# Normalising with the mean itself in place of its negative, in a fused attention and expert layer

## The chip, the cores and the metric

The kernel runs on one core of one Trainium2 chip. The time is the device time of one execution in microseconds (us), and smaller is better. The core has five engines with instruction queues of their own: PE (TensorE, matrix products), DVE (VectorE), ACT (ScalarE), POOL (GpSimd) and SP (SyncE, here a DMA queue only). They meet in semaphores: an instruction can wait until a semaphore has reached a value, and add to one when it ends.

## The reference

One layer for 8 sequences of 512 tokens with 256 features, float32. The attention is unusual: the softmax weights of a token are multiplied by its own value row, so their sum, computed as a ratio that is close to 1, scales the value rows. The feed-forward part picks one of 8 low-rank adapters per token. There are four normalisations without weights.

```python
def _layernorm(x, axis=-1, eps=1e-05):
    m = jnp.mean(x, axis=axis, keepdims=True)
    v = jnp.var(x, axis=axis, keepdims=True)
    return (x - m) / jnp.sqrt(v + eps)

# attention (16 heads)
att = jax.nn.softmax(jnp.einsum('blhd,bmhd->blmh', q, k) * scale, axis=2)
opt = jnp.einsum('blmh,blhd->blhd', att, v).reshape(b, l, d)
return opt @ w_out.T + b_out

# feed-forward: for each expert i of 8, masked to the tokens whose gate picks it
lora = jnp.einsum('bsr,fr->bsf', jnp.einsum('bsd,rd->bsr', x, lora_A[i]), lora_B[i])
inter = jax.nn.relu(base + lora)
expert_out = jnp.einsum('bsf,df->bsd', inter, wo_W) + wo_b

# the layer
x = x + _layernorm(attn(_layernorm(x)))
x = x + _layernorm(ffn(_layernorm(x)))
```

## The kernel before

A batch is one sequence: 4 tiles (t) of 128 tokens by 256 features. The program is a pipeline over 8 batches, written out by hand for each engine. In batch b every engine goes through 32 slots. A slot is one pair of score tiles: PE multiplies (L222) two 128x512 tiles into two of five PSUM banks (`ps`), DVE takes the negative row maximum (L722), ACT does the exponential and its sum (L511). Between the slots stand pieces of the other stages, for batches b+1 (projections), b-1 and b-2 (what follows the attention). Large products are made of three float32 rounded ones, from a high and a low part of each operand (`three`, L189). PE works strictly in the order of its program, with three further banks (`pu`).

The normalisations are shared out. DVE computes mean and variance per token: `bn_stats` by tile (L758) and `bn_aggr` (L763), into `mv[n][:, t, 0]` (mean) and `mv[n][:, t, 1]` (variance). POOL then runs `spread` (L996): it writes the negative mean into `nmr[n][:, 0]` (L1001), the variance plus epsilon into `nmr[n][:, 1]` (L1002), and that to the power -0.5 into `nmr[n][:, 2]` (L1004). After it `norm` (L1007) works tile by tile: (src + negative mean) * power, with both as per-partition scalars (L1010). One spread serves two or four tiles.

Norm 0 is that of x (`x_norm`, giving `xn`), 1 that of the attention's output (`y_norm`, added to `xb` by L1016), 2 that of the sum (`sum_norm`, giving `y`), 3 that of the feed-forward output (`y2_norm`). In each batch POOL's order (L1138) is: scale the value rows `vo` of batch b-1 by the ratio that DVE made from the finished exponentials (L1047), two low parts of `inter` (L1079, L1081), `x_norm(b+1)`, `y_norm(b-1)` for tiles 0, 1 and then 2, 3, `sum_norm(b-1)` in the same halves, bias additions, the mask of the gate, `y2_norm(b-2)`, two more low parts.

Who waits for these norms: PE transposes the result of norm 2 in `y_t` (L276) at slot 14, by the helper at L227, ahead of all later work in its queue, and ACT and DVE make high and low parts from it (L544, L726). DVE's statistics of the sum wait for POOL's additions (L797). In the last batch `y_half` (L343) does the transposes by half batches (L336), the norms of its second half and of the end are done by DVE itself (L880, L883), and only their spreads stay on POOL (L1148 to L1150); DVE waits for them. In the first batch DVE and POOL share the spread of norm 0 (L896, L1117), and DVE subtracts the mean (L899).

Of the kernel before, what the change touches and what calls it, by code (L numbers as in the profile page):

```python
# [8 lines left out]
ALU = mybir.AluOpType  # L9
# [4 lines left out]
NT = L // 128  # L14
EPS = 1e-5
# [17 lines left out]
def sandwich(nc, x, wqk, wv, bqk, wout, wgate, wi, lora, wib, wo, bfree, bg, ident, out):  # L33
    with ExitStack() as ctx:
        def sb(name, shape, dt=F32):
            return ctx.enter_context(nc.sbuf_tensor(name, shape, dt))

        def sem(name):
            return ctx.enter_context(nc.semaphore(name))
# [4 lines left out]
        xb = sb("xb", [128, XB, NT, D])  # L44
        xn = sb("xn", [128, NT, D])
# [24 lines left out]
        halves = sb("halves", [128, NT])  # L70
# [4 lines left out]
        sone = sb("sone", [128, NT, H])  # L75
        st6 = [sb(f"st6_{i}", [128, NT, 6]) for i in range(3)]
        mv = [sb(f"mv_{i}", [128, NT, 2]) for i in range(3)]
        nmr = [sb(f"nmr_{i}", [128, 3, NT]) for i in range(3)]
        gs = sb("gs", [128, NT, 40])
        g8 = sb("g8", [128, 6, NT, E])  # L80
        g1 = sb("g1", [128, 5, NT])
# [45 lines left out]
        rstd = [sem(f"rstd{i}") for i in range(4)]  # L127
# [589 lines left out]
        def vector(e):  # L717
# [160 lines left out]
                whole_stats(3, 2, B - 1, (t,))  # L878

            def norm(i, n, dst, src, b, ts):  # L880
                e.wait_ge(rstd[i], (6 if i in (1, 2) else 3) * b + 3 + 3 * (ts[0] // len(ts)))
                for t in ts:
                    e.tensor_scalar(dst[:, t, :], src[:, t, :], nmr[n][:, 0, t:t + 1], nmr[n][:, 2, t:t + 1], ALU.add,  # L883
                                    ALU.mult).then_inc(normed[i], 1)

            def add(i, src, b, ts):
# [6 lines left out]
                tile_stats(0, 0, xb[:, 0], t)  # L893
            whole_stats(0, 0, 0, ALL)
            e.wait_ge(stats[0], 8)
            e.tensor_scalar(nmr[0][:, 1, :], mv[0][:, :, 1], EPS, None, ALU.add).then_inc(rstd[0], 2)  # L896
            e.wait_ge(rstd[0], 3)
            for t in ALL:
                e.tensor_scalar(xn[:, t, :], xb[:, 0, t, :], mv[0][:, t, 0:1], nmr[0][:, 2, t:t + 1], ALU.subtract,  # L899
                                ALU.mult).then_inc(normed[0], 1)  # L900
            e.wait_ge(bqk_loaded, 16)
            e.tensor_scalar(bqk_s[:, 0:2], bqk_s[:, 0:2], 0.25, None, ALU.mult).then_inc(qk_split, 1)
# [44 lines left out]
            b = B - 1  # L947
# [34 lines left out]
            slot(29)  # L982
            slot(30), ratio_half(1), gate_half(1, 0), gate_half(2, 0)
            slot(31), project(b, 1), gate_half(3, 0), y_stats(b, HALVES[1]), norm(1, 1, y, y, b, HALVES[1])
            add(1, y, b, HALVES[1]), sum_stats(b, HALVES[1]), norm(2, 1, y, xb[:, b % XB], b, HALVES[1])
            y_half(1), gate_half(1, 1), gate_half(2, 1), gate_half(3, 1), f1_half(0, 0), f1_half(0, 1)
            y2_stats(b - 1, HALVES[0]), f1_half(0, 2), f1_half(0, 3), f1_half(1, 0), y2_stats(b - 1, HALVES[1])
            f1_half(1, 1), f1_half(1, 2), f1_half(1, 3), last_stats(0), last_stats(1), last_stats(2)
            norm(3, 2, y2, y2, b, (0,)), add(3, y2, b, (0,)), norm(3, 2, y2, y2, b, (1,)), add(3, y2, b, (1,))
            last_stats(3), norm(3, 2, y2, y2, b, (2,)), add(3, y2, b, (2,)), norm(3, 2, y2, y2, b, (3,))  # L990
            add(3, y2, b, (3,))
# [3 lines left out]
        def pool(e):  # L995
            def spread(i, n, b, ts=ALL):  # L996

                s = slice(ts[0], ts[-1] + 1)
                k = (6 if i in (1, 2) else 3) * b + 3 * (ts[0] // len(ts))
                e.wait_ge(stats[i], 8 * b + 2 * ts[-1] + 2)  # L1000
                e.tensor_scalar(nmr[n][:, 0, s], mv[n][:, s, 0], -1.0, None, ALU.mult).then_inc(rstd[i], 1)  # L1001
                e.tensor_scalar(nmr[n][:, 1, s], mv[n][:, s, 1], EPS, None, ALU.add).then_inc(rstd[i], 1)  # L1002
                e.wait_ge(rstd[i], k + 2)
                e.tensor_tensor(nmr[n][:, 2, s], nmr[n][:, 1, s], halves[:, s], ALU.pow).then_inc(rstd[i], 1)  # L1004
                return k + 3

            def norm(i, n, dst, src, b, ts=ALL):  # L1007
                e.wait_ge(rstd[i], spread(i, n, b, ts))
                for t in ts:
                    e.tensor_scalar(dst[:, t, :], src[:, t, :], nmr[n][:, 0, t:t + 1], nmr[n][:, 2, t:t + 1], ALU.add,  # L1010
                                    ALU.mult).then_inc(normed[i], 1)

            def add(i, src, b, ts=ALL):
# [24 lines left out]
            def x_norm(b):  # L1038
                if here(b):
                    if b:  # L1040
                        e.wait_ge(xnT_ps, 2 * b)
                    norm(0, 0, xn, xb[:, b % XB], b)
# [41 lines left out]
            def y_norm(b, ts):  # L1084
                if here(b):
                    norm(1, 1, y, y, b, ts), add(1, y, b, ts)

            def sum_norm(b, ts):
                if here(b):
                    norm(2, 1, y, xb[:, b % XB], b, ts)  # L1090
# [22 lines left out]
            for i in range(PIECES):  # L1113
                e.memset(stack[:, i, 0:2].rearrange("p q c l -> p (q c l)").bitcast(F32), 0.0).then_inc(zeroed, 1)
            e.wait_ge(const_set, CONSTS)
            e.wait_ge(rstd[0], 2)
            e.tensor_tensor(nmr[0][:, 2, :], nmr[0][:, 1, :], halves[:], ALU.pow).then_inc(rstd[0], 1)  # L1117
            e.wait_ge(normed[0], 4)
            first_piece(e, 0, 1)
            first_piece(e, 1, 1)  # L1120
# [21 lines left out]
            b = B - 1  # L1142
# [3 lines left out]
            v_bias(b), scale_half(0), y2_bias(b - 2, 1), mask(b - 1), y2_norm(b - 2), y_norm(b, HALVES[0])  # L1146
            f1_lows(b - 1, 0, 0), sum_norm(b, HALVES[0]), f1_lows(b - 1, 0, 1), f1_lows(b - 1, 1, 0)
            scale_half(1), f1_lows(b - 1, 1, 1), mask_half(0), spread(1, 1, b, HALVES[1])  # L1148
            spread(2, 1, b, HALVES[1]), y2_bias(b - 1, 0), mask_half(1), y2_bias(b - 1, 1), y2_norm(b - 1)
            spread(3, 2, b, (0,)), spread(3, 2, b, (1,)), spread(3, 2, b, (2,)), spread(3, 2, b, (3,))  # L1150

# [84 lines left out]
        @block.vector  # L1236
        def _(e):
            vector(e)

        @block.gpsimd  # L1240
        def _(e):
            pool(e)
# [50 lines left out]
```

## Time and profile before

| | us |
|---|---|
| median of 3 runs | 541.47 |
| lowest and highest | 539.78, 541.62 |
| the profiled execution | 541.58 |
| its span, first to last instruction | 539.8 |

| engine | busy us | share | instructions |
|---|---|---|---|
| PE | 508.2 | 94% | 2721 |
| DVE | 463.9 | 86% | 991 |
| ACT | 453.5 | 84% | 1238 |
| POOL | 368.7 | 68% | 557 |

All rows come from the one profiled execution. A row "A <- B" says that A stood idle until B ended. "issue" in a chain is time in which an engine waited for nothing that the profile shows, such as the gap between two instructions that follow each other. "xN" behind an operation merges N instructions in sequence, and the time is that of them all. The mean granted TensorE clock is 0.991 of full speed. Consecutive matmuls overlap, and their ends are modelled.

### The profile page before, as it was taken

The numbers are of one execution on the slowest core, as the hardware profiler recorded it, in microseconds if no ns is written. First come the engines' busy times: TensorE is split into PE (matmuls) and PEld (weight loads), VectorE is DVE, ScalarE is ACT, GpSimd is POOL, SyncE is SP. The second block draws the span as 40 slices with busy tenths as digits, with TensorE's granted clock in tenths as the row PEclk, the third lists the DMA queues.
The fourth block names the chain that finished last, engine by engine and source line by source line (L and its number), as shares of the span: only waits on it lengthen the run. The fifth ranks groups of instructions, "written<-read, shape, count | busy, mean of one in ns | idle before, by whom it ended". The sixth has DMA issues, their size and how long they took to land.

```text
span 539.8 us, 8865 instructions
## 1 busy us (share of the span) xinstructions
PE 508.2 (94%) x2721; PEld 403.4 (75%) x2721; DVE 463.9 (86%) x991; ACT 453.5 (84%) x1238; POOL 368.7 (68%) x557
## 2 busy tenths in 40 slices
PE   8999988999999999999999999999999998798995
PEld 6765544588887789677877788778878787577995
DVE  4598999988999899998999899998999789975455
ACT  2499988999889998999889998999889988893220
POOL 5696046417992898559991998379873987797263
PEclk9989999999999999999999999999999999998998
DMA  7693453035310625045411633053403640310002
GB/s 240 187 251 92 110 125 79 1 88 147 76 42 2 166 74 153 1 109 126 118 40 34 172 76 111 0 148 88 118 1 80 156 117 1 78 40 1 1 2 79
DMA packets 22645, 47.63 MB, mean 88 GB/s; under 512 B 5220, under 2 KB 13540, under 8 KB 21958
## 3 DMA queue, kind: packets, MB, share of 16 engines
q1 hardware_dynamic: 21910, 45.95, 32.0%
q0 software_dynamic: 256, 0.52, 0.4%
q10 hardware_dynamic: 432, 0.59, 0.3%
q8 instruction: 22, 0.36, 0.3%
q14 instruction: 25, 0.20, 0.1%
HBM read 8.24 MB, written 4.19 MB: 23 GB/s over the span
## 4 chain that ended last, share of the span: by engine, by line
POOL 32%; PE 29%; ACT 24%; DVE 7%; issue 5%; POOLq 0%; ACTq 0%
ACT ps L511 17%; PE pu L193 15%; POOL y L1010 7%; PE ps L222 6%; POOL nmr L1004 5%; POOL inter L1081 5%; POOL xb L1016 4%; PE ps L193 3%; POOL vo L1047 3%; DVE nmax L722 3%; ACT qk L525 3%; POOL xn L1010 2%; POOL inter L1079 2%; POOL nmr L1002 2%; POOL nmr L1001 2%
## 5 line engine op out<-in xcount | busy, mean ns | idle before, releaser
L511 ACT ACTIVATE ps<-ps,nmax 128x512 f32<-128x512 f32 x512 | 344.7, 699 | 20.2 <-DVE nmax L722 19.8
L722 DVE TENSOR_REDUCE nmax<-ps 128x1 f32<-128x512 f32 x512 | 320.0, 679 | 25.9 <-PE ps L222 24.6
L222 PE MATMUL ps<-stack 128*128 128x512 f32 x512 | 176.8, 420 | 3.6 <-ACT ps L511 2.6
L511 ACT ACTIVATION_READ_ACCUMULATOR ps<-ps,nmax 128x1 f32 x512 | 125.9, 246 | 0.0
L222 PEld LDWEIGHTS ps<-stack 128*128 128x128 f32 x512 | 94.2, 190 | 36.1 <-ACT ps L511 23.1
L193 PE MATMUL pu<-yT,wi_r 128*128 128x512 f32 x336 | 87.9, 397 | 0.0
L193 PE MATMUL pu<-wo_r,inter 128*128 128x256 f32 x624 | 80.9, 282 | 0.0
L193 PEld LDWEIGHTS pu<-wo_r,inter 128*128 128x128 f32 x624 | 78.9, 188 | 2.6
L193 PEld LDWEIGHTS pu<-yT,wi_r 128*128 128x128 f32 x336 | 62.8, 188 | 13.5
L1081 POOL TENSOR_TENSOR inter<-y,inter 128x1024 fp32r<-128x1024 f32 x26 | 62.1, 2387 | 2.1
L200 PE MATMUL ps<-ones_r 128*128 128x512 f32 x115 | 48.6, 470 | 6.8 <-ACT ps L511 5.6
L193 PE MATMUL pu<-xnT,wqk_r 128*128 128x512 f32 x192 | 49.5, 395 | 0.7 <-DVE xnT L726 0.7
L200 PEld LDWEIGHTS ps<-ones_r 128*128 128x128 f32 x115 | 23.0, 202 | 31.2 <-ACT ps L511 25.2
L1024 POOL TENSOR_TENSOR ml<-gs,g 128x128 f32<-128x128 f32 (+1 forms) x9 | 3.5, 389 | 62.2 <-DVE g L865 62.2
L1004 POOL TENSOR_TENSOR nmr<-nmr,halves 128x2 f32<-128x2 f32 (+2 forms) x50 | 39.8, 796 | 4.2
L1016 POOL TENSOR_TENSOR xb<-xb,y 128x256 f32<-128x256 f32 x58 | 41.1, 735 | 1.8
L193 PEld LDWEIGHTS pu<-xnT,wqk_r 128*128 128x128 f32 x192 | 35.5, 188 | 8.2 <-issue 1.1
L1047 POOL TENSOR_TENSOR vo<-vo,sone 128x256 f32<-128x256 f32 x32 | 18.9, 623 | 29.0 <-DVE sone L816 24.7
L271 PE MATMUL pu<-wout_s,oT 128*128 128x256 f32 x128 | 34.5, 395 | 2.3 <-ACT oT L581 1.6
L1001 POOL TENSOR_SCALAR nmr<-mv 128x2 f32<-128x2 f32 (+2 forms) x50 | 12.0, 240 | 33.0 <-DVE mv L763 29.9
L1079 POOL CAST inter<-y 128x1024 fp32r<-128x1024 f32 x26 | 27.0, 1039 | 10.6 <-ACT y L576 10.6
L576 ACT ACTIVATE y<-pu 128x512 f32<-128x512 f32 x52 | 33.8, 677 | 0.1
(130 smaller groups left out, 685.2 us busy)
## 6 DMA issues: line engine op xcount, KB each, us to landing
stack<-qk SPq DMA_DIRECT2D x256, 128.0 KB, 2.5
xb<-in_x SPq DMA_DIRECT2D x7, 512.0 KB, 4.9
out_y<-xb SPq DMA_DIRECT2D x7, 512.0 KB, 3.6
xb<-in_wo SPq DMA_DIRECT2D x1, 1024.0 KB, 7.6
vo<-in_wi SPq DMA_DIRECT2D x2, 512.0 KB, 6.8
oT<-in_wqk ACTq DMA_DIRECT2D x1, 512.0 KB, 4.1
xb<-in_x SPq DMA_DIRECT2D x4, 128.0 KB, 4.1
stack<-qk SPq DMA_DIRECT2D x8, 64.0 KB, 2.4
```

What stands on the lines that cost most here:

```text
L193: p = e.matmul(out_, lT(a, c), r(b_, c), start=first and n == 0 and j == 0, stop=last and n == len(chunks) - 1 and j == 2)
L200: e.matmul(bank[:].rearrange("p (k m) -> p k m", k=4), ones_r[:], ones_r[:].unsqueeze(1).to_broadcast([128, 4, 128]), start=True, stop=True)
L222: e.matmul(ps[i % NS][:], st[:, 1 - p, c, t * 128:(t + 1) * 128], st[:, 2, c, :], start=True, stop=True).then_inc(scored, 1)
L271: p = e.matmul(o, oT[:, c, t * 128:(t + 1) * 128], wout_s[:, c, :], start=c == 0, stop=c == 1)
L511: e.activation(ps[i % NS][:], ps[i % NS][:], ACT.Exp, bias=nmax[:, i % 8:i % 8 + 1], accum_out=ssum[:, b % 2, t, h:h + 1]).then_inc(exped, 1)
L722: e.tensor_reduce(nmax[:, i % 8:i % 8 + 1], ps[i % NS][:], AX_X, ALU.max, negate=True).then_inc(maxed, 1)
L1004: e.tensor_tensor(nmr[n][:, 2, s], nmr[n][:, 1, s], halves[:, s], ALU.pow).then_inc(rstd[i], 1)
L1010: e.tensor_scalar(dst[:, t, :], src[:, t, :], nmr[n][:, 0, t:t + 1], nmr[n][:, 2, t:t + 1], ALU.add, ALU.mult).then_inc(normed[i], 1)
L1016: e.tensor_tensor(xb[:, b % XB, t, :], xb[:, b % XB, t, :], src[:, t, :], ALU.add).then_inc(added[i], 1)
L1047: e.tensor_tensor(vt, vt, sone[:, t, :].unsqueeze(2).to_broadcast([128, H, 16]), ALU.mult).then_inc(scaled, 1)
L1079: e.tensor_copy(high, whole).then_inc(f1_pool_high, 1)
L1081: e.tensor_tensor(inter[:, 1, f:f + 2, :], whole, high.bitcast(F32), ALU.subtract).then_inc(f1_pool_low, 1)
```

## The change

POOL no longer writes the negative mean. `nmr` has two rows in place of three (variance plus epsilon, power), each spread has two operations in place of three, and the norms on POOL and on DVE's tail take `mv[n][:, t, 0:1]` as their first scalar and subtract. The semaphore values of `rstd` follow: two steps per spread in place of three.

```diff
-        nmr = [sb(f"nmr_{i}", [128, 3, NT]) for i in range(3)]
+        nmr = [sb(f"nmr_{i}", [128, 2, NT]) for i in range(3)]
...
             def norm(i, n, dst, src, b, ts):
-                e.wait_ge(rstd[i], (6 if i in (1, 2) else 3) * b + 3 + 3 * (ts[0] // len(ts)))
+                e.wait_ge(rstd[i], (4 if i in (1, 2) else 2) * b + 2 + 2 * (ts[0] // len(ts)))
                 for t in ts:
-                    e.tensor_scalar(dst[:, t, :], src[:, t, :], nmr[n][:, 0, t:t + 1], nmr[n][:, 2, t:t + 1], ALU.add,
+                    e.tensor_scalar(dst[:, t, :], src[:, t, :], mv[n][:, t, 0:1], nmr[n][:, 1, t:t + 1], ALU.subtract,
                                     ALU.mult).then_inc(normed[i], 1)
...
-            e.tensor_scalar(nmr[0][:, 1, :], mv[0][:, :, 1], EPS, None, ALU.add).then_inc(rstd[0], 2)
-            e.wait_ge(rstd[0], 3)
+            e.tensor_scalar(nmr[0][:, 0, :], mv[0][:, :, 1], EPS, None, ALU.add).then_inc(rstd[0], 1)
+            e.wait_ge(rstd[0], 2)
...
             def spread(i, n, b, ts=ALL):
 
                 s = slice(ts[0], ts[-1] + 1)
-                k = (6 if i in (1, 2) else 3) * b + 3 * (ts[0] // len(ts))
+                k = (4 if i in (1, 2) else 2) * b + 2 * (ts[0] // len(ts))
                 e.wait_ge(stats[i], 8 * b + 2 * ts[-1] + 2)
-                e.tensor_scalar(nmr[n][:, 0, s], mv[n][:, s, 0], -1.0, None, ALU.mult).then_inc(rstd[i], 1)
-                e.tensor_scalar(nmr[n][:, 1, s], mv[n][:, s, 1], EPS, None, ALU.add).then_inc(rstd[i], 1)
-                e.wait_ge(rstd[i], k + 2)
-                e.tensor_tensor(nmr[n][:, 2, s], nmr[n][:, 1, s], halves[:, s], ALU.pow).then_inc(rstd[i], 1)
-                return k + 3
+                e.tensor_scalar(nmr[n][:, 0, s], mv[n][:, s, 1], EPS, None, ALU.add).then_inc(rstd[i], 1)
+                e.wait_ge(rstd[i], k + 1)
+                e.tensor_tensor(nmr[n][:, 1, s], nmr[n][:, 0, s], halves[:, s], ALU.pow).then_inc(rstd[i], 1)
+                return k + 2
 
             def norm(i, n, dst, src, b, ts=ALL):
                 e.wait_ge(rstd[i], spread(i, n, b, ts))
                 for t in ts:
-                    e.tensor_scalar(dst[:, t, :], src[:, t, :], nmr[n][:, 0, t:t + 1], nmr[n][:, 2, t:t + 1], ALU.add,
+                    e.tensor_scalar(dst[:, t, :], src[:, t, :], mv[n][:, t, 0:1], nmr[n][:, 1, t:t + 1], ALU.subtract,
                                     ALU.mult).then_inc(normed[i], 1)
```

POOL's program around `x_norm` and the first half of `y_norm`, before; the shapes are partitions x elements of what is written:

```order
L1001 TENSOR_SCALAR nmr<-mv 128x4 [waits stats0,xnT_ps]
L1002 TENSOR_SCALAR nmr<-mv 128x4
L1004 TENSOR_TENSOR nmr<-nmr,halves 128x4 [waits rstd0]
L1010 TENSOR_SCALAR xn<-xb,nmr 128x256 [waits rstd0]
L1010 TENSOR_SCALAR xn<-xb,nmr 128x256 x3
L1001 TENSOR_SCALAR nmr<-mv 128x2 [waits stats1]
L1002 TENSOR_SCALAR nmr<-mv 128x2
L1004 TENSOR_TENSOR nmr<-nmr,halves 128x2 [waits rstd1]
L1010 TENSOR_SCALAR y<-y,nmr 128x256 [waits rstd1]
L1010 TENSOR_SCALAR y<-y,nmr 128x256
```

The same place now (all lines from here on are one lower):

```order
L1001 TENSOR_SCALAR nmr<-mv 128x4 [waits stats0,xnT_ps]
L1003 TENSOR_TENSOR nmr<-nmr,halves 128x4 [waits rstd0]
L1009 TENSOR_SCALAR xn<-xb,mv,nmr 128x256 [waits rstd0]
L1009 TENSOR_SCALAR xn<-xb,mv,nmr 128x256 x3
L1001 TENSOR_SCALAR nmr<-mv 128x2 [waits stats1]
L1003 TENSOR_TENSOR nmr<-nmr,halves 128x2 [waits rstd1]
L1009 TENSOR_SCALAR y<-y,mv,nmr 128x256 [waits rstd1]
L1009 TENSOR_SCALAR y<-y,mv,nmr 128x256
```

L1001 is now the addition of epsilon, which was L1002, and takes over the wait for DVE's statistics. The norm reads `mv` beside `nmr`. POOL's program has 50 instructions fewer; no other order changes. At its end, where DVE waits for the spread of each of the last four tiles, it was

```order
L1001 TENSOR_SCALAR nmr<-mv 128x1 [waits stats3]
L1002 TENSOR_SCALAR nmr<-mv 128x1
L1004 TENSOR_TENSOR nmr<-nmr,halves 128x1 [waits rstd3]
L1001 TENSOR_SCALAR nmr<-mv 128x1 [waits stats3]
L1002 TENSOR_SCALAR nmr<-mv 128x1
L1004 TENSOR_TENSOR nmr<-nmr,halves 128x1 [waits rstd3]
```

and is now

```order
L1001 TENSOR_SCALAR nmr<-mv 128x1 [waits stats3]
L1003 TENSOR_TENSOR nmr<-nmr,halves 128x1 [waits rstd3]
L1001 TENSOR_SCALAR nmr<-mv 128x1 [waits stats3]
L1003 TENSOR_TENSOR nmr<-nmr,halves 128x1 [waits rstd3]
```

so that the power is the second instruction after the wait instead of the third.

## Rows read from the trace of the kernel before

**Rows 1.** The profile's page, parts 1 and 4: busy time by engine; shares of the chain.
```profile
PE 508.2 (94%) x2721; PEld 403.4 (75%) x2721; DVE 463.9 (86%) x991; ACT 453.5 (84%) x1238; POOL 368.7 (68%) x557
...
POOL 32%; PE 29%; ACT 24%; DVE 7%; issue 5%; POOLq 0%; ACTq 0%
```

**Rows 2.** The chain that ended last, 190 to 250 us: start, length (us), what.
```profile
191.18 2.36 POOL vo L1047 x4
...
200.51 0.24 POOL nmr L1001
200.76 0.09 issue
200.84 0.25 POOL nmr L1002
...
215.52 0.23 POOL nmr L1001
...
216.97 1.11 POOL y L1010 x2
218.08 0.14 issue
```

**Rows 3.** PE in order of time, three stretches: start, length (us), line, operation.
```profile
216.27 1.10 PE L222 MATMUL ps<-stack 128*128 128x512 f32 x4
218.21 1.06 PE L227 MATMUL pu<-id_s,y 128*128 128x128 f32 x8 [0.85 <-POOL y L1010]
...
483.02 0.63 PE L336 MATMUL pu<-id_s,y 128*128 128x128 f32 x4 [0.20 <-POOL y L1010]
...
505.20 0.63 PE L336 MATMUL ps<-id_s,y 128*128 128x128 f32 x4 [0.35 <-DVE y L883]
```

**Rows 4.** Who waited for whom: total us, times, longest.
```profile
PE pu L227 <- POOL y L1010: 5.0, 7, 0.9
```

**Rows 5.** One line's instructions: the POOL operation that negates the mean, ns min/median/max.
```profile
L1001 POOL TENSOR_SCALAR nmr<-mv x50: 221/239/297, 33.0 to 535.0; 128x2 f32<-128x2 f32 x32, 128x4 f32<-128x4 f32 x14, 128x1 f32<-128x1 f32 x4
```

**Rows 6.** DVE in order of time, two stretches of the same batch.
```profile
206.95 0.25 DVE L763 BATCH_NORM_AGGREGATE mv<-st 128x2 f32<-128x6 f32 x2
...
212.15 0.43 DVE L758 BATCH_NORM_STATS2 st<-xb 128x6 f32<-128x256 f32 x1 [0.40 <-POOL xb L1016]
212.83 0.43 DVE L758 BATCH_NORM_STATS2 st<-xb 128x6 f32<-128x256 f32 x1 [0.26 <-POOL xb L1016]
213.29 0.25 DVE L763 BATCH_NORM_AGGREGATE mv<-st 128x2 f32<-128x6 f32 x2
```

**Rows 7.** Busy us (x count) of PE, PEld, DVE, ACT, POOL, one batch's period; then clock.
```profile
190.24:249.53 59.29, 58.06 (x319) 47.20 (x318) 55.16 (x119) 55.93 (x155) 45.15 (x67) 1.00 0.34 90
```

**Rows 8.** The end of the chain, from 535 us: start, length (us), what.
```profile
535.00 0.28 POOL nmr L1001
...
535.36 0.38 POOL nmr L1002
...
535.78 0.61 POOLq L34
...
536.41 0.42 DVE y L883
```

**Rows 9.** DVE in order of time, near the end.
```profile
535.24 0.42 DVE L889 TENSOR_TENSOR xb<-xb,y 128x256 f32<-128x256 f32 x1
```

**Rows 10.** POOL's groups by shape: busy us, mean ns, idle before.
```profile
L1081 POOL TENSOR_TENSOR inter<-y,inter 128x1024 fp32r<-128x1024 f32 x26 | 62.1, 2387 | 2.1
L1016 POOL TENSOR_TENSOR xb<-xb,y 128x256 f32<-128x256 f32 x58 | 41.1, 735 | 1.8
L1010 POOL TENSOR_SCALAR y<-y,nmr 128x256 f32<-128x256 f32 x58 | 31.7, 559 | 2.4
...
L1106 POOL TENSOR_TENSOR wi_r<-vo,wi_r 128x512 fp32r<-128x512 f32 x4 | 5.0, 1282 | 0.0
```

**Rows 11.** ACT in order of time, at the eviction of yT.
```profile
218.88 1.09 ACT L544 ACTIVATE yT<-pu 128x512 fp32r<-128x512 f32 x2 [0.97 <-PE pu L227]
```

More of the change, by code:

```diff
@@ L895, in vector @@
             e.wait_ge(stats[0], 8)
-            e.tensor_scalar(nmr[0][:, 1, :], mv[0][:, :, 1], EPS, None, ALU.add).then_inc(rstd[0], 2)
-            e.wait_ge(rstd[0], 3)
+            e.tensor_scalar(nmr[0][:, 0, :], mv[0][:, :, 1], EPS, None, ALU.add).then_inc(rstd[0], 1)
+            e.wait_ge(rstd[0], 2)
             for t in ALL:
-                e.tensor_scalar(xn[:, t, :], xb[:, 0, t, :], mv[0][:, t, 0:1], nmr[0][:, 2, t:t + 1], ALU.subtract,
+                e.tensor_scalar(xn[:, t, :], xb[:, 0, t, :], mv[0][:, t, 0:1], nmr[0][:, 1, t:t + 1], ALU.subtract,
                                 ALU.mult).then_inc(normed[0], 1)
@@ L1115, in pool @@
             e.wait_ge(const_set, CONSTS)
-            e.wait_ge(rstd[0], 2)
-            e.tensor_tensor(nmr[0][:, 2, :], nmr[0][:, 1, :], halves[:], ALU.pow).then_inc(rstd[0], 1)
+            e.wait_ge(rstd[0], 1)
+            e.tensor_tensor(nmr[0][:, 1, :], nmr[0][:, 0, :], halves[:], ALU.pow).then_inc(rstd[0], 1)
             e.wait_ge(normed[0], 4)
```

## The prediction

> **What bounds the kernel now.** I read the page's shares first. PE is busy for 94% of the span, and yet the chain that ended last lies on POOL for 32% of it, more than on any other engine [rows 1]. So PE is nearly full, but something on POOL is waited for. The next view is therefore the chain in order of time, over one batch in the middle of the run (190 to 250 us). It lies on POOL without a break from the scaling of vo at 191.18 to the last normalised y tile: 216.97 + 1.11 = 218.08 us, and then 0.14 us to PE [rows 2]. After that it goes through ACT and PE to the next scaling of vo at 250.48, so one period is about 59.3 us. The third view is PE in order of time around the hand-over: PE's score matmuls end at 217.37 (216.27 + 1.10), and its transposes of y start at 218.21, after 0.85 us of idle time that POOL's norm ended [rows 3]. The list of waits has the same stall for the whole run: 7 times, 5.0 us, 0.9 at most [rows 4]. Two more such stalls stand in the last batch, where the program uses the half transposes: 0.20 us at 483.02 and 0.35 us at 505.20, the last one behind a norm on DVE that itself waits for POOL's statistics [rows 3].
>
> So two loops of nearly equal length run side by side. The one through POOL is now the longer by 0.85 us per batch. The other is PE's own work.
>
> **What the change removes.** It takes out the operation that negates the mean, 50 times [rows 5]. One costs 0.24 us of busy time, but what the chain loses is the distance from its start to the start of the next operation: 200.84 - 200.51 = 0.33 us with the 0.09 us of issue behind it [rows 2]; over the spreads of one batch it is 0.32 on average. The 50 of them are 16 us of POOL's time. Most of this is worth nothing by itself, since only five of the six per batch lie between the scaling of vo and the transposes of y: one of x_norm, two of y_norm, two of sum_norm. They make 5 x 0.325 = 1.62 us, and the norm that PE waits for ends at 218.08 - 1.62 = 216.46 us in place of 218.08, or 216.60 at PE.
>
> Does each of the five count in full? The first operation of a spread waits for DVE's statistics, so POOL could arrive too early. The last spread is the tightest. POOL comes to it at 215.52 now and would come at 215.52 - 4 x 0.325 = 214.22. The aggregates it reads are done at 213.29 + 0.25 = 213.54 [rows 2, 6], which leaves 0.68 us, and they come earlier too, as DVE's statistics there waited 0.40 and 0.26 us for POOL's additions [rows 6]. For the second half of y they are done at 206.95 + 0.25 = 207.20 [rows 6], and POOL comes to that spread at about 208.1. So no new wait for DVE appears, and all 1.62 us arrive.
>
> **What is late next.** PE gets to the transposes at 217.37 and POOL's tile would be there at 216.60. The stall of 0.85 us goes wholly, and 0.77 us of POOL's saving is over. From here PE decides. Its busy time in this period of 59.29 us is 58.06 [rows 7], so 1.23 us is all the idle time it has, 0.85 of them this stall. The gain of a batch is therefore at least 0.85 us, if PE's own loop is untouched, and at most 1.23 us. For the part above 0.85 speaks that DVE no longer stands 0.66 us at its statistics [rows 6], so that ACT gets its maxima sooner and PE its free banks; against it that PE runs nearly back to back before 217.37. I take it close to the lower end, 0.07 us in each of five steady batches, 0.35 us in all; the ends are 0 and 5 x 0.38 = 1.9 us.
>
> **The last batch.** The two stalls of the half transposes are 0.20 and 0.35 us [rows 3]. POOL saves three spreads ahead of the first and DVE's norms get theirs two spreads sooner (0.65 us) ahead of the second, so both go, and no more than the stall does, 0.55 us together. At the very end nothing runs beside the chain: POOL negates the mean at 535.00, starts the epsilon operation at 535.36, then the power, and DVE's norm starts at 536.41 [rows 8]. The removed step is worth 535.36 - 535.00 = 0.36 us if the rest keeps its length. The epsilon operation took 0.38 us there, against 0.25 in the middle of the run [rows 2, 8], while DVE's addition with two operands in SBUF ran at 535.24 to 535.66 [rows 9]. With the step gone, it is the power that starts beside that addition and may be stretched in the same way. I take 0.30, with ends at 0.1 and 0.4.
>
> The Trainium skill has a rule for this (SBUF — State Buffer, Who interferes with whom): a DVE instruction with two SBUF inputs contends with a GpSimd instruction that reads SBUF. By that rule the power would be held until 535.66, and the final step would bring about 0.1 us less than 0.36; without it all 0.36. Either leaves the forecast where it is.
>
> **Other edits, at nothing.** The norms read the mean where DVE wrote it, still a per-partition scalar, and subtract in place of adding: same count, same shapes. The buffer of statistics gets smaller. On DVE the first batch's semaphore steps change by number only. No DMA and no instruction of PE, ACT, DVE or SP moves.
>
> **The sum.** 5.0 (seven stalls) + 0.35 (relief) + 0.55 (half transposes) + 0.30 (end) = 6.2 us. The profiled execution took 541.58 us, 0.1 us above the median of 541.47, so 541.58 - 6.2 = 535.4 us. By the bounds alone it runs from 5.0 + 0 + 0.55 + 0.1 = 5.65 to 5.0 + 1.9 + 0.55 + 0.4 = 7.85 us of gain: 535.9 to 533.7. Three runs of the same kernel here lie 1.8 us apart, which I add on either side.
>
> **Rivals.**
> (a) The subtraction costs more on POOL than the addition. No row shows POOL's two-step operation with a subtraction. For equal cost speaks that its two-operand subtraction goes by 2387 - 1282 = 1105 ns for 512 more elements, 2.16 ns each; from 1282 ns at 512 that line gives 730 ns at 256, and the addition of 256 took 735 [rows 10]. Twelve normalised tiles lie in the POOL stretch, so the change would lose from 1.62 / 12 = 0.135 us more per tile, 24% over the 559 ns of now [rows 10]. If the tile cost what the two-operand form costs, 735 in place of 559 ns, 12 x 0.176 = 2.11 us would come against 1.62 saved: 0.49 us longer in each of the six to seven periods, some 3 us in all, 544.5 us. Slower than before. The lower bound is no difference.
> (b) Another engine takes most of the stall. ACT stands 0.97 us before the eviction of y [rows 11] and then runs without idle time, and the chain goes over ACT's exponentials until about 228 us. If these hold PE back as soon as it comes earlier, half of the 5.0 us comes: 2.5 + 0.55 + 0.3 = 3.3 us, 538.3 us. Against it: ACT's queue starts at that eviction, and moves with it.
> (c) All of POOL's saving arrives: five batches at 1.62, 0.4 and 0.3 for the first and the last stall, 0.85 for the end: 9.7 us, 531.9 us. This needs PE to arrive 0.77 us sooner as well, and PE has 0.38 us of other idle time per batch [rows 7], so its busy time would have to hide waits.
>
> **Chances.** The forecast (533.7 to 537.5) 0.70; (b) 0.14; (c) 0.07; (a) 0.06; 0.03 for what I do not see. The measurement tells 0.5%, 2.7 us, from no change: faster is below 538.8 us. The forecast, (c) and nearly half to two thirds of (b) lie there: 0.86. Within 0.5%: the rest of (b) and the cheap end of (a), 0.09. Slower: 0.05. For 8 in 10 I go from 533.0 to 538.9 us, which takes in the forecast and most of (b) and leaves out (a) and (c).
>
> **What would show it.** The wait of PE's transposes for POOL's norm falls from 5.0 us to under 0.5. The distance between two scalings of vo falls from 59.3 to 58.3 or 58.4 us. POOL's busy time falls by 12 us and its normalised tiles stay at 0.56 us; at over 0.69 us I would be wrong by (a). DVE's waits for POOL's additions (0.40, 0.26) vanish. If PE's wait for POOL goes and the period stays above 58.9, it is (b), and a new wait of PE for ACT must show. If POOL waits for DVE's aggregates inside the stretch, my margins of 0.7 us were wrong.

## The result

The changed kernel takes 602.66 us (median of 4 runs, 600.23 to 604.06) against 541.37 us for the kernel before (539.78 to 541.62). The ratio is 1.113, with a 95% interval of 1.110 to 1.115. My forecast was 535.4 us, in a range of 533.0 to 538.9 us, with 0.05 for any slowdown. It missed by 67 us, on the wrong side. The medians below leave out two executions that lie far from the others of their kernels, 700.27 us (mean granted clock 0.65) where DVE negates and 2828.37 us where PE is kept busy.

From the page of the changed kernel: busy time by engine, and the chain's shares, which answer to [rows 1].

```profile
PE 530.2 (88%) x2721; PEld 413.9 (69%) x2721; DVE 469.2 (78%) x991; ACT 456.9 (76%) x1238; POOL 433.4 (72%) x507
...
POOL 47%; PE 20%; DVE 17%; ACT 10%; issue 5%; POOLq 0%; ACTq 0%
```

POOL has 50 instructions fewer and 64.7 us more busy time (433.4 against 368.7). The groups by shape say where it went (busy us, mean ns; idle before); they answer to [rows 10].

```profile
L1009 POOL TENSOR_SCALAR y<-y,mv,nmr 128x256 f32<-128x256 f32 x58 | 70.5, 1227 | 2.3
L1080 POOL TENSOR_TENSOR inter<-y,inter 128x1024 fp32r<-128x1024 f32 x26 | 62.0, 2384 | 2.1
L1015 POOL TENSOR_TENSOR xb<-xb,y 128x256 f32<-128x256 f32 x58 | 41.1, 736 | 1.8
L1009 POOL TENSOR_SCALAR y<-xb,mv,nmr 128x256 f32<-128x256 f32 x30 | 36.6, 1228 | 1.6
L1009 POOL TENSOR_SCALAR xn<-xb,mv,nmr 128x256 f32<-128x256 f32 x28 | 34.0, 1227 | 0.7
```

The norm itself went from 559 ns a tile to 1227, while the other large operations on POOL kept their length (2384 against 2387 ns, 736 against 735). There are 116 such tiles: 116 x 0.668 = 77 us more, less 12 us for the removed operations. The waits, PE in order of time at the hand-over, and one batch's period answer to [rows 4], [rows 3] and [rows 7]:

```profile
PEld ps L222 <- ACT ps L511: 47.6, 94, 1.8
ACT ps L511 <- DVE nmax L722: 44.9, 29, 3.9
DVE nmax L722 <- PE ps L222: 37.2, 53, 2.6
...
DVE st L758 <- POOL xb L1015: 27.0, 25, 3.0
...
PE pu L227 <- POOL y L1009: 20.1, 7, 4.1
...
ACT y L576 <- POOL xb L1015: 6.0, 5, 1.2
```

```profile
238.51 1.07 PE L227 MATMUL pu<-id_s,y 128*128 128x128 f32 x8 [2.74 <-POOL y L1009]
239.33 2.81 PE L193 MATMUL pu<-xnT,wqk_r 128*128 128x512 f32 x6
241.93 1.05 PE L222 MATMUL ps<-stack 128*128 128x512 f32 x2
```

```profile
205.62:274.18 68.56, 62.28 (x320) 49.36 (x319) 56.32 (x119) 56.59 (x155) 54.28 (x61) 0.95 0.30 78
```

PE's wait for POOL's norm did not fall from 5.0 us to nothing, it grew to 20.1. DVE's statistics, which waited 0.40 and 0.26 us for POOL in one batch, now wait up to 3.0 us at a time, and the row maxima stand behind them in DVE's queue. ACT has a wait for POOL's additions that the kernel before has not (6.0 us, 5 times). The distance between two scalings of vo is 68.6 us instead of 59.3.

### The profile page after: what moved, and what is told of

Its sections match the earlier page's. It is cut to its first block, busy times and chain, and to the rows that moved or that the text cites. A ratio compares the mean times of both kernels' runs of the same rounds, so it can differ in the third digit from the quotient of the medians.

```text
span 602.3 us, 8814 instructions
## 1 busy us (share of the span) xinstructions
PE 530.2 (88%) x2721; PEld 413.9 (69%) x2721; DVE 469.2 (78%) x991; ACT 456.9 (76%) x1238; POOL 433.4 (72%) x507
## 4 chain that ended last, share of the span: by engine, by line
POOL 47%; PE 20%; DVE 17%; ACT 10%; issue 5%; POOLq 0%; ACTq 0%
POOL y L1009 17%; PE pu L193 9%; DVE nmax L722 8%; ACT ps L511 7%; POOL xb L1015 6%; POOL nmr L1003 6%; POOL xn L1009 5%; POOL inter L1080 4%; PE ps L193 4%; POOL vo L1046 3%; PE ps L222 2%; PE pu L227 2%; DVE qk L736 2%; POOL inter L1078 2%; POOL nmr L1001 2%
## 5 line engine op out<-in xcount | busy, mean ns | idle before, releaser
L222 PE MATMUL ps<-stack 128*128 128x512 f32 x512 | 185.8, 428 | 22.2 <-ACT ps L511 22.0
L222 PEld LDWEIGHTS ps<-stack 128*128 128x128 f32 x512 | 95.8, 192 | 61.8 <-ACT ps L511 47.6
L511 ACT ACTIVATION_READ_ACCUMULATOR ps<-ps,nmax 128x1 f32 x512 | 119.2, 233 | 0.0
L193 PEld LDWEIGHTS pu<-wo_r,inter 128*128 128x128 f32 x624 | 80.6, 192 | 2.4
L1009 POOL TENSOR_SCALAR y<-y,mv,nmr 128x256 f32<-128x256 f32 x58 | 70.5, 1227 | 2.3
L1080 POOL TENSOR_TENSOR inter<-y,inter 128x1024 fp32r<-128x1024 f32 x26 | 62.0, 2384 | 2.1
L193 PE MATMUL pu<-xnT,wqk_r 128*128 128x512 f32 x192 | 56.1, 436 | 0.7 <-DVE xnT L726 0.7
L758 DVE BATCH_NORM_STATS2 st<-xb 128x6 f32<-128x256 f32 x64 | 24.7, 418 | 31.8 <-POOL xb L1015 27.0
L193 PEld LDWEIGHTS pu<-xnT,wqk_r 128*128 128x128 f32 x192 | 40.3, 214 | 9.9 <-issue 1.1
L1009 POOL TENSOR_SCALAR y<-xb,mv,nmr 128x256 f32<-128x256 f32 x30 | 36.6, 1228 | 1.6
```

The costliest lines, as they stand in the source:

```text
L193: p = e.matmul(out_, lT(a, c), r(b_, c), start=first and n == 0 and j == 0, stop=last and n == len(chunks) - 1 and j == 2)
L222: e.matmul(ps[i % NS][:], st[:, 1 - p, c, t * 128:(t + 1) * 128], st[:, 2, c, :], start=True, stop=True).then_inc(scored, 1)
L511: e.activation(ps[i % NS][:], ps[i % NS][:], ACT.Exp, bias=nmax[:, i % 8:i % 8 + 1], accum_out=ssum[:, b % 2, t, h:h + 1]).then_inc(exped, 1)
L758: e.bn_stats(st6[n][:, t, :], src[:, t, :]).then_inc(stats[i], 1)
L1009: e.tensor_scalar(dst[:, t, :], src[:, t, :], mv[n][:, t, 0:1], nmr[n][:, 1, t:t + 1], ALU.subtract, ALU.mult).then_inc(normed[i], 1)
L1080: e.tensor_tensor(inter[:, 1, f:f + 2, :], whole, high.bitcast(F32), ALU.subtract).then_inc(f1_pool_low, 1)
```

## Experiments

**Which of the two edits of the norm is dear?** The norm changed in two ways: its first scalar comes from `mv`, and it subtracts. The first kernel has the second alone, the second kernel the first alone.

```diff
(from the kernel before)
-                e.tensor_scalar(nmr[n][:, 0, s], mv[n][:, s, 0], -1.0, None, ALU.mult).then_inc(rstd[i], 1)
+                e.tensor_scalar(nmr[n][:, 0, s], mv[n][:, s, 0], 1.0, None, ALU.mult).then_inc(rstd[i], 1)
...
-                    e.tensor_scalar(dst[:, t, :], src[:, t, :], nmr[n][:, 0, t:t + 1], nmr[n][:, 2, t:t + 1], ALU.add,
+                    e.tensor_scalar(dst[:, t, :], src[:, t, :], nmr[n][:, 0, t:t + 1], nmr[n][:, 2, t:t + 1], ALU.subtract,
```

> The kernel before, with its three operations per spread, but the first copies the mean (times 1.0) in place of negating it, and the norms on POOL and DVE subtract what it wrote. Result unchanged. Theory S (POOL's two-step operation is slow with a subtraction in it, wherever the scalar comes from): a normalised tile takes 1.23 us as in the changed kernel, and since POOL is then the only bound, the 50 extra operations of 0.32 us come on top of 602.7 us where they lie on POOL's loop (6 per batch, 7 batches, 14 us): about 616 us. Theory O (reading the mean where DVE wrote it, in pairs with the variance, is what is slow): a tile stays at 0.56 us and the time at 541.4.

Measured: 624.66 us, ratio 1.153 (1.151 to 1.156). A tile takes 1.23 us with the scalar in `nmr`, where it always was. So it is the subtraction. I had expected 616; of the 9 us between, about half are accounted for below.

```diff
(from the changed kernel, on POOL and in DVE's tail)
-                    e.tensor_scalar(dst[:, t, :], src[:, t, :], mv[n][:, t, 0:1], nmr[n][:, 1, t:t + 1], ALU.subtract,
+                    e.tensor_scalar(dst[:, t, :], src[:, t, :], mv[n][:, t, 0:1], nmr[n][:, 1, t:t + 1], ALU.add,
```

> The changed kernel with an addition in place of the subtraction in the norms of POOL and of DVE's tail: two operations per spread, mean read in place, but it adds the mean where it should subtract it, so the values are others. Theory S: a tile takes 0.56 us, and the time is what I forecast for the change itself, 535.2 us (6.2 less than 541.4), with the wait of PE's transposes for POOL gone. Theory O: a tile takes 1.23 us and the time stays at 602. If S holds but the wait of PE turns into another one, 538.3.

Measured: 534.53 us, ratio 0.987 (0.985 to 0.988). This kernel differs from the changed one by one word in two places, and by 68 us; it adds the mean where it should subtract it, so its result is wrong and it serves the measurement alone. It is also the test of all the rest of my forecast. POOL's tile (group by shape) and PE at the hand-over (in order of time):

```profile
L1009 POOL TENSOR_SCALAR y<-y,mv,nmr 128x256 f32<-128x256 f32 x58 | 31.7, 559 | 2.3
```

```profile
214.63 1.09 PE L222 MATMUL ps<-stack 128*128 128x512 f32 x4
215.55 1.03 PE L227 MATMUL pu<-id_s,y 128*128 128x128 f32 x8
```

The transposes of y start without a wait (no row `PE pu L227 <- POOL y` is left in the list), and the scalings of vo stand at 247.92 and 306.27 us, 58.35 us apart. Reading the mean in place costs nothing.

**What else is dear on POOL?** Two kernels run the kernel before and then, with the other engines idle, forms of the operation on scratch, such as

```diff
+            for i in range(4):
+                e.tensor_scalar(to[:, 256 * i:256 * i + 256], src[:, 0:256], n_m, r, ALU.subtract, ALU.mult).then_inc(bench, 1)
```

> The kernel before, and after its last work, with all engines idle, POOL runs fifteen forms of elementwise operation on scratch, two or four times each (lines 1159 to 1201). Theory S: with both scalars per partition at 256 elements, addition and multiplication takes 0.56 us whether the first scalar is nmr's or mv's, and subtraction and multiplication 1.23; at 512 elements the two differ by 1.3 us. Theory O: mv's scalar alone makes it 1.23. A rival C, that it is contention with DVE and not the operation: all forms of 256 elements take 0.56 here. Open: whether a lone subtraction, a subtraction as the second step, an immediate, or another operation such as max or mult twice is slow too.

The groups by shape of the appended lines. 1159 is add, mult with nmr's scalar; 1162 the same with mv's; 1165 subtract, mult; 1168 and 1171 these two at 512 elements; 1174 and 1177 a lone add and a lone subtract; 1198 the two-operand subtract:

```profile
L1165 POOL TENSOR_SCALAR xn<-vo,nmr 128x256 f32<-128x256 f32 x4 | 4.9, 1228 | 0.1
...
L1171 POOL TENSOR_SCALAR xn<-vo,nmr 128x512 f32<-128x512 f32 x2 | 4.1, 2075 | 0.1
L1174 POOL TENSOR_SCALAR xn<-vo,nmr 128x256 f32<-128x256 f32 x4 | 3.7, 933 | 0.1
L1177 POOL TENSOR_SCALAR xn<-vo,nmr 128x256 f32<-128x256 f32 x4 | 3.6, 926 | 0.1
L1198 POOL TENSOR_TENSOR xn<-vo 128x256 f32<-128x256 f32 x4 | 2.8, 725 | 0.1
...
L1159 POOL TENSOR_SCALAR xn<-vo,nmr 128x256 f32<-128x256 f32 x4 | 2.2, 558 | 1.0 <-DVE xb L890 1.0
...
L1162 POOL TENSOR_SCALAR xn<-vo,mv,nmr 128x256 f32<-128x256 f32 x4 | 2.2, 557 | 0.1
L1168 POOL TENSOR_SCALAR xn<-vo,nmr 128x512 f32<-128x512 f32 x2 | 1.5, 772 | 0.1
```

It needs no contention: the same 1228 ns with DVE at rest. The surprise is the lone step. One addition takes 933 ns, longer than an addition and a multiplication together, 558.

> The kernel before, and eleven more forms of POOL's elementwise operation on scratch after its end (lines 1158 to 1192). Theory F, from the first fifteen forms: two steps that are each an addition or a multiplication go a fast way (0.56 us at 256 elements), everything else a slow one, a lone step too (0.93). So addition twice should take 0.56, addition then subtraction, subtraction twice, min or max 1.2, a lone multiplication 0.93, and at 128 elements the fast form 0.45 and the slow 0.80 by the slopes of 0.84 and 3.3 ns an element. Rival: the fast way belongs to pairs with a multiplication alone; then addition twice takes 1.2.

1162 is subtract, mult at 128 elements, 1159 add, mult at 128; 1168 add, add; 1165 a lone multiplication:

```profile
L1168 POOL TENSOR_SCALAR xn<-vo,nmr 128x256 f32<-128x256 f32 x4 | 4.9, 1228 | 0.1
...
L1165 POOL TENSOR_SCALAR xn<-vo,nmr 128x256 f32<-128x256 f32 x4 | 3.6, 924 | 0.1
...
L1162 POOL TENSOR_SCALAR xn<-vo,nmr 128x128 f32<-128x128 f32 x4 | 3.2, 801 | 0.1
...
L1159 POOL TENSOR_SCALAR xn<-vo,nmr 128x128 f32<-128x128 f32 x4 | 1.7, 448 | 1.0 <-DVE xb L890 1.0
```

Both kernels together, mean ns of one on POOL with per-partition scalars at 128x256 where nothing else is said:

| form | ns |
|---|---|
| add, mult; mult, add; mult, mult | 558, 558, 559 |
| subtract, mult; mult, subtract | 1228, 1225 |
| add, add; add, subtract; subtract, subtract | 1228, 1223, 1222 |
| max, mult; min, mult; mult, max | 1221, 1218, 1222 |
| lone add, subtract, mult | 933, 926, 924 |
| immediates: add, mult; subtract, mult; lone add | 407, 1073, 851 |
| two operands: subtract, add, mult | 725, 722, 724 |

So my first reading, that any pair of additions and multiplications is fast, fell: addition twice is slow, as the rival of that run had it. The two lengths at 128 elements came as expected (448 and 801 ns against 0.45 and 0.80 us). Three pairs are fast, and each has a multiplication and otherwise an addition or another multiplication. The fast pair costs (772 - 558) / 256 = 0.84 ns an element, the slow one (2075 - 1228) / 256 = 3.3. Why these three, the traces do not say.

**Which tiles lie on the loop?** The changed kernel, with the norm of the feed-forward output back to negating and adding:

```diff
             def y2_norm(b):
                 if here(b):
-                    norm(3, 2, y2, y2, b), add(3, y2, b)
+                    e.wait_ge(stats[3], 8 * b + 8)
+                    e.tensor_scalar(neg[:], mv[2][:, :, 0], -1.0, None, ALU.mult).then_inc(neg_set, 1)
+                    k = spread(3, 2, b)
...
+                        e.tensor_scalar(y2[:, t, :], y2[:, t, :], neg[:, t:t + 1], nmr[2][:, 1, t:t + 1], ALU.add,
+                                        ALU.mult).then_inc(normed[3], 1)
```

> The changed kernel, but the norm of the feed-forward output (four of the sixteen tiles of a batch) negates the mean again and adds. Theory: these tiles lie on POOL's loop too, because the two low parts and the scaling of vo stand behind them, so each batch gets 4 x 0.668 - 0.325 = 2.35 us back, 16 us in seven batches: about 586 us. Rival, as my forecast counted: only the twelve tiles between the scaling of vo and the transposes of y count: no change, 602.7 us.

Measured: 585.77 us, ratio 1.083 (1.079 to 1.087), the sum that the theory had. The rival is out: the four tiles count too. But the parts are not the theory's, and that they add up to its 16 us is in part luck. In the profiled executions the seven distances between scalings of vo fell by 0.5, 2.1, 3.4, 3.4, 3.4, 2.1 and 0.0 us, not by 2.35 each, and another 4.1 us fell away behind the last scaling. The 2.1 is the tiles; where it is 3.4, PE's clock did not fall behind the transposes either (see below). That the four tiles come almost whole could be read in the kernel before. POOL in order of time:

```profile
247.86 2.40 POOL L1081 TENSOR_TENSOR inter<-y,inter 128x1024 fp32r<-128x1024 f32 x1
250.48 1.78 POOL L1047 TENSOR_TENSOR vo<-vo,sone 128x256 f32<-128x256 f32 x3 [0.23 <-DVE sone L816]
```

POOL's last low part ended at 250.25 us and the scaling of vo started at 250.48, so the norm ahead of the low parts had little room: 0.2 us here, and 0.2 us in which POOL waited for ACT between the two low parts. In the changed kernel ACT waits for the additions behind these tiles (the row of 6.0 us above), and DVE's ratio ahead of the scaling (L816) lasts 1.18 to 1.20 us in place of 0.30 in the last five batches, until just after POOL's last low part.

**The clock's part.** The changed kernel, and PE works instead of standing still ahead of its wait:

```diff
                     bank = banks[take(("yT", b, c), yT_low, 2 * b + c + 1)]
+                    if c == 0:
+                        run_idle(bank, 12)
                     e.wait_ge(normed[2], 4 * b + 4)
```

> The changed kernel, and PE runs 12 idle matmuls (2.8 us) on the bank it has taken, ahead of its wait for POOL's y tiles. Result unchanged. Theory K: part of the 61 us is TensorE's clock: after the stall of 2.7 us the first six matmuls of the next projection take 2.56 us where they took 1.40, granted clock 0.77 in that stretch, so with PE kept busy 1.2 us come back in each batch that has it, 5 to 8 us in all: about 596 us. Rival: the clock costs nothing, since POOL is the bound and has slack ahead of its next work there: 602.7 us.

Measured: 597.69 us, ratio 1.104 (1.101 to 1.107), 5 us under the changed kernel. (The 1.40 and 2.56 us in the expectation are the pieces of the chain; PE in order of time has 1.64 us for the same six matmuls in the kernel before and 2.81 in the stretch shown above.) A run for the profile:

> The same kernel as the one in which PE is kept busy ahead of its wait, for a profile. Theory K: the six matmuls after the transposes of y take 1.4 us, the granted clock stays at 1.00 in that stretch, and the period is about 1 us shorter than the 68.6 us of the changed kernel.

It took 598.54 us. In order of time on PE, to be laid beside the changed kernel's stretch above:

```profile
235.26 2.90 PE L200 MATMUL pu<-ones_r 128*128 128x512 f32 x12
238.00 1.04 PE L227 MATMUL pu<-id_s,y 128*128 128x128 f32 x8
238.79 1.63 PE L193 MATMUL pu<-xnT,wqk_r 128*128 128x512 f32 x6
```

The six matmuls behind the transposes take 1.63 us, against 2.81 after a stall of 2.74 us. The granted clock over 237 to 246 us was 1.00 here. In the changed kernel it was 0.77 over 238.5 to 246, a part of it at the lower of the two levels:

```profile
238.50:246.00 7.50, 7.49 (x30) 5.73 (x31) 4.61 (x8) 6.17 (x16) 5.42 (x8) 0.77 0.00 0
```

In four of the five steady batches the distance between scalings fell from 68.6 to between 67.1 and 67.3 us, in one only to 68.4. That one is the batch shown: there the granted clock was 0.50 from 227.6 to 234.4 us, ahead of the idle matmuls, which therefore started late and ended after POOL's last y tile (236.61 us), so that they themselves held the transposes back.

The kernel with the feed-forward norm restored shows the clock's price without idle matmuls. In two of its steady batches the six matmuls behind the transposes took 2.91 and 2.54 us, at a granted clock of 0.77 and 0.79 around them, and the distance was 66.5 us. In the three others they took 1.64 us at 1.00, and it was 65.2. So the lower clock there costs 1.3 us. A fall ahead of the transposes, where PE has a wait for POOL to lose, costs next to nothing: with PE kept busy the batch with the clock at 0.51 from 296.0 to 299.4 us is 67.2 us long, and two without such a fall are 67.1.

**Can the saving be had without the subtraction?** Where DVE itself norms, subtraction should cost nothing. The kernel before with only those six spreads shortened, and DVE's norm reading and subtracting the mean (shown is POOL's part):

```diff
-                e.tensor_scalar(nmr[n][:, 0, s], mv[n][:, s, 0], -1.0, None, ALU.mult).then_inc(rstd[i], 1)
+                if negate:
+                    e.tensor_scalar(nmr[n][:, 0, s], mv[n][:, s, 0], -1.0, None, ALU.mult).then_inc(rstd[i], 1)
```

> The kernel before, changed only where DVE does the norm: the last six spreads lose the negation and DVE subtracts the mean in place (six tiles). POOL's norms stay as before. Result unchanged. Theory: DVE's subtraction costs what its addition does (0.41 us a tile in both traces), so the end of the chain gets the 0.35 us before the last half transposes and 0.1 to 0.36 us at the very end: 541.4 - 0.6 = 540.8 us, which this measurement hardly tells from no change. Rival: subtraction is dear on DVE too: slower, by 1 us or more.

Measured: 540.55 us, ratio 0.999 (0.998 to 1.0005): no difference that can be told. DVE's norm took 409 ns a tile in the changed kernel with the subtraction against 406 before.

Next, DVE negates the mean for POOL, and POOL adds:

```diff
(from the changed kernel, in whole_stats)
+                e.wait_ge(stats[i], 8 * b + 2 * ts[-1] + 2)
+                s = slice(ts[0], ts[-1] + 1)
+                e.tensor_scalar(mv[n][:, s, 0], mv[n][:, s, 0], -1.0, None, ALU.mult).then_inc(negated[i], 1)
```

> The changed kernel, but DVE negates the mean in place right after its aggregates (one more operation of DVE per whole_stats), POOL's norms add, and only where DVE norms itself (first batch, end of the last) it subtracts. Result unchanged. Theory: subtraction is dear on POOL alone, so this keeps what the removal is worth (534.5 us in the version that adds the mean) and pays about 0.2 to 0.3 us of DVE six times a batch, most of it beside PE, which is then the bound: 535.5 us, range 534.5 to 538. Rival: DVE's extra operations delay the row maxima and so ACT and PE, 6 x 0.3 us in seven batches: 547 us.

Measured: 548.89 us, ratio 1.015 (1.013 to 1.017), 14 us above the version that adds the mean. Close to the rival, but not for its reason, as the profile shows. A run for the profile:

> The same kernel as the one in which DVE negates by tensor_scalar, for a profile at TensorE's full clock. Theory L: many of the 51 negations last 0.5 to 2.4 us, as long as the POOL instruction beside them, about 14 us together on the path; rival D: nearly all last 0.17 us.

It took 547.18 us. DVE around its first negation, in order of time, and then POOL in the same stretch:

```profile
26.30 0.38 DVE L767 BATCH_NORM_AGGREGATE mv<-st 128x2 f32<-128x6 f32 x4
26.71 6.25 DVE L772 TENSOR_SCALAR mv<-mv 128x4 f32<-128x4 f32 x1
32.88 4.35 DVE L726 TENSOR_REDUCE nmax<-ps 128x1 f32<-128x512 f32 x7
```

```profile
25.77 2.28 POOL L1114 CAST wo_r<-xb 128x512 fp32r<-128x512 f32 x4
28.02 4.91 POOL L1117 TENSOR_TENSOR wo_r<-xb,wo_r 128x512 fp32r<-128x512 f32 x4
33.14 0.23 POOL L1013 TENSOR_SCALAR nmr<-mv 128x4 f32<-128x4 f32 x1 [0.21 <-DVE mv L772]
```

A negation of four numbers a partition, 0.17 us elsewhere, lasted 6.25 us: until POOL's row of casts and subtractions, without a gap between them, was through at 32.93. Theory L held for this one, but not for its "many": of 51, one lasted 6.25 us and fourteen 0.33 to 0.64, each of which ended 0.02 to 0.03 us after the POOL instruction beside it. The one long wait weighs most: the first scaling of vo stands at 79.59 us here and at 73.09 in the next kernel, 6.5 of the 8.3 us between the spans of the two profiled executions (545.4 and 537.1). The Trainium skill has a rule for this (SBUF — State Buffer, Who interferes with whom): a tensor_scalar can enter a mode that takes the port pair shared with GpSimd, and of two such instructions the one that issued second is blocked until the other has ended; a tensor_reduce on trn2 never contends. The trace agrees with the first half, except that the wait lasted through seven POOL instructions in a row, where the page speaks of one, and the next run agrees with the second half.

```diff
-                e.tensor_scalar(mv[n][:, s, 0], mv[n][:, s, 0], -1.0, None, ALU.mult).then_inc(negated[i], 1)
+                e.tensor_reduce(mv[n][:, s, 0], mv[n][:, s, 0:1], AX_X, ALU.max, negate=True).then_inc(negated[i], 1)
```

> As the version in which DVE negates, but the negation is a tensor_reduce over one element with the output negated, in place of a tensor_scalar. Result unchanged. Theory L: the tensor_scalar of two floats waited until a POOL instruction that ran at the same time ended (0.73 us against 0.17), and with it the row maxima behind it in DVE's queue; a reduction does not wait (the row maxima, 0.67 us, are reductions and keep their length beside POOL), so each negation costs 0.2 to 0.3 us of DVE and the time is 535.5 us, range 534.5 to 538. Rival D: it is the number of DVE's operations and their waits that cost: 548.9 us as there.

Measured: 539.07 us, ratio 0.997 (0.996 to 0.998): 9.8 us better by the operation alone, and a little under the kernel before. The line of the negation (ns minimum, median, maximum):

```profile
L772 DVE TENSOR_REDUCE mv<-mv x51: 154/155/159, 26.4 to 517.3; 128x2 f32<-128x2 f32 x44, 128x4 f32<-128x4 f32 x7
```

None waited. But I had expected 535.5. The scalings of vo stand 58.83 us apart (249.97 and 308.80), 0.48 more than in the version that adds the mean: six negations a batch, each with its wait for the aggregates, cost that much together; which part of them does, I have not shown. Fewer of them:

```diff
(in whole_stats, from the kernel in which only DVE's norms subtract)
+                if i == 2 and not (b == B - 1 and ts[0] == 2):
...
+                    e.tensor_reduce(mv[n][:, s, 0], mv[n][:, s, 0:1], AX_X, ALU.max, negate=True).then_inc(negated, 1)
```

> From the kernel before: DVE negates by a reduction for the two halves of the norm of the sum alone, whose POOL tiles then add the mean from mv; the other POOL spreads negate as before; where DVE norms itself it subtracts. Result unchanged. Theory: PE's stall was 0.85 us a batch, and each spread without the negation gives POOL 0.41 us, so two of them take nearly all of it, while DVE pays for two negations in place of six (each 0.08 us of the period by 58.82 against 58.35 us). The period should be about 58.5 us and the time 537.5 us, 1.5 under the version with all six. Rival: all of POOL's saving is needed, because it also frees DVE's statistics of their waits; then 539 us or more.

Measured: 539.21 us, ratio 0.994 (0.993 to 0.996) against a kernel before at 541.91 in that comparison. It beats both kernels; whether it beats the version with six negations the overlapping intervals do not say. The scalings stand 58.94 us apart (249.72 and 308.66), not 58.5. PE's wait for the norm is down to 0.2 us, once; DVE's statistics still wait 2.1 us in all, 0.5 of it in the batch from 190 to 250 us:

```profile
DVE st L759 <- POOL xb L1026: 2.1, 9, 0.3
```

So the rival of that run has the better part of it, though I have not shown that these waits are the whole of the missing 0.4 us.

## Why the prediction was wrong

**The step that failed.** "Other edits, at nothing", and behind it rival (a) with its price. I took the cost of POOL's two-step operation with a subtraction from POOL's two-operand subtraction, which does cost what an addition costs (725 and 722 ns), and took the two-operand form, 735 ns, for what a tile would take if I was wrong. Neither bound a form that no row showed. The measured tile is 1227 ns, 0.668 us more. The break-even that I worked out, 0.135 us more per tile, gave the right side; the chance of 0.06 for the rival and its size (544.5 us) rested on that analogy.

**The account of a batch.** The removed operation gave more than 0.325 us: the stretch from the scaling of vo to the transposes of y was 27.03 us (218.21 - 191.18) and is 32.89 (238.51 - 205.62). Twelve tiles bring 12 x 0.668 = 8.02; so five spreads gave 8.02 - 5.86 = 2.16 us, 0.43 each, since a gap of 0.09 us ahead of the first operation of a spread went too. The rest of the loop brings four tiles of the feed-forward norm less a spread, 4 x 0.668 - 0.43 = 2.24, and the slower matmuls behind the stall, 2.81 - 1.63 = 1.18. Together 5.86 + 2.24 + 1.18 = 9.28 us, and the period grew by 68.6 - 59.3 = 9.3. The kernel with the copied mean checks it: 59.3 + 16 x 0.668 + 1.18 = 71.2 us, and its scalings stand 71.2 us apart (282.13 and 353.29 us). That is also half of why it took 8.7 us more than I expected: I had put 0.32 for 0.43 on a spread, which is 4 to 5 us over 42 spreads. Most of the rest I had not counted at all: in the profiled executions 2.7 us came behind the last scaling of vo and 0.7 ahead of the first.

**What held.** All that I said of the removal itself, as the version with the addition shows. PE's stall went (5.0 us to no row), the period fell to 58.35 us (I had 58.3 to 58.4), no new wait of POOL for DVE's aggregates appeared in the stretch of a steady batch (three new ones of 0.17 to 0.68 us stand outside), and the sum was 6.2 us against 541.66 - 534.53 = 7.1 measured in that comparison. Rivals (b) and (c) are out. The batches came as forecast: between the first and the last scaling of vo the version with the addition is 387.34 - 382.02 = 5.3 us shorter, and I had 5.0 + 0.35 (a steady batch gave 59.30 - 58.35 = 0.95 us against my 0.85 + 0.07). The missing 0.9 us lies at the two ends: 0.3 us ahead of the first scaling, for which I had nothing, and 1.6 us behind the last, where I had 0.55 + 0.30. One sum of mine does not come out: 1.8 us on either side of 533.7 to 535.9 gives 531.9 to 537.7, not the 533.7 to 537.5 beside the chance of 0.70. It changes nothing in the miss.

**The end of the chain.** I took 0.30 for the last spread, for fear of the power being stretched. It was stretched, and the 0.30 came. The chain of the version with the addition ends

```profile
528.10 0.28 POOL nmr L1001
528.38 0.04 issue
528.42 0.77 POOLq L34
```

and the part behind the epsilon operation lasts 0.77 us where it lasted 0.61 [rows 8]. In return the epsilon operation, no longer beside DVE's addition, takes 0.28 us in place of 0.38. From POOL's first operation to DVE's norm it is 529.22 - 528.10 = 1.12 us, against 536.41 - 535.00 = 1.41 [rows 8]: 0.29 us gained. That a DVE instruction with two SBUF inputs contends with a GpSimd one that reads SBUF is the rule of the Trainium skill (SBUF — State Buffer, Who interferes with whom) that the prediction cites. The trace agrees in kind: beside DVE's addition of 528.34 to 528.77 us the power itself took 0.72 us, against 0.56 alone.

**The count of tiles.** Had I priced rival (a) rightly at 1.23 us, twelve tiles would have given 59.3 + 5.9 = 65.2 us a batch (with the 0.43 us of a spread that the runs showed; 65.7 with my 0.325); the kernel with the feed-forward norm restored has just that (333.67 - 268.48 = 65.2). The four tiles that I left out (2.1 to 2.2 us) and the clock (1.2 to 1.3) are the other 3.4 us.

## What to carry to other kernels

An edit that swaps the operation of an instruction is not free because its count and shape stay. If no row shows this engine with this pair of operations, its cost is unknown: price the break-even, and measure the form by itself before anything is built on it. On POOL keep per-partition scaling and shifting in an add and mult pair, and let an engine that does not mind the subtraction have it. When an engine becomes later, read how much room it had at each of its hand-overs, not only at the one that bounds now. Of a small operation that is moved to DVE ask which form does not wait for POOL.

## What the runs showed of the hardware

- POOL's tensor_scalar has a fast way for three pairs (add, mult; mult, add; mult, mult): 558 ns for 128x256 float32. All other pairs tried took 1218 to 1228 ns, and a lone step 924 to 933, more than a fast pair.
- With immediates in place of per-partition scalars the fast pair took 407 ns and the slow one 1073.
- DVE's tensor_scalar on four floats per partition waited 6.25 us, through seven POOL instructions in a row; the same work as a tensor_reduce took 154 to 159 ns, 51 times out of 51.
- After a stall of 2.74 us PE's next six matmuls took 2.81 us; with idle matmuls in the stall 1.63. In the kernel with the feed-forward norm restored they took 1.64 after a stall of 2.53 us (granted clock 1.00). In the last batch the six matmuls behind the half transposes took 2.74 us after a stall of 1.78 us in the changed kernel, and 1.64 after one of 1.80 us in the kernel with the feed-forward norm restored. So the stall's length does not settle by itself whether the clock falls.
- A lower clock is paid for by its place: 1.3 us a batch where it fell behind the transposes (66.5 against 65.2 us), 0.1 us at most where it fell ahead of PE's wait for POOL (67.2 to 67.3 against 67.1 us with PE kept busy).
